# Two attention heads side by side on TensorE, the rope's swap of neighbours by DMA, and the causal mask filled into the probabilities by GpSimd

## What is computed

```python
# layer 0: deformable 3x3 convolution: 9 taps, each a bilinear sample at an offset that a 3x3 convolution gives
sampled = bilinear_sample(x, ys, xs)
out = einsum('bkhwc,ock->bohw', sampled, w) + bias
# layer 1: causal attention, 16 heads of 64, over the 1024 tokens of an image, with rope on q and k
q, k = apply_rope(x @ w_q.T), apply_rope(x @ w_k.T)      # pairs (a, b) -> (a*c - b*s, a*s + b*c)
out = softmax(mask(q @ k.T / 8)) @ v @ w_o.T
# layer 2: spectral filters (16 causal convolutions) and a mix of experts
```

## Time and profile before

| | |
|---|---|
| median of 3 runs | 3925.68 us (3906.31 to 3928.64) |
| span of the profiled execution | 3932.8 us |
| its offsets and convolution stages | up to about 290 us |
| its attention stage | about 292 to 3114 us |
| its spectral stage | from about 3118 us to the end |
| busy share of the span | PE 86%, DVE 63%, POOL 43%, ACT 37% |

### The profile page before, as it was taken

How to read it: one execution, slowest core, us unless ns; L and a number is a source line. 1 busy time by engine, 2 the same in 40 slices (tenths; PEclk the granted TensorE clock), 3 DMA queues, 4 the chain that set the end, 5 groups by cost and what they waited for, 6 DMA issues and landing times. The chain is left out here.

```text
span 3932.8 us, 69093 instructions
## 1 busy us (share of the span) xinstructions
PE 3385.7 (86%) x21387; PEld 2365.0 (60%) x21387; DVE 2484.0 (63%) x4247; ACT 1442.3 (37%) x2188; POOL 1702.7 (43%) x1424
## 2 busy tenths in 40 slices
PE   6336999999999999999999999999999569999998
PEld 1124555555555555555555555555555359898887
DVE  2346666676666767666766766667676556464646
ACT  0002333333333333333333333333333235454545
POOL 0464555555555555555555555555555320000000
PEclk8557999999999999999999999999999779999999
DMA  2524454445545544444554445455555624333333
GB/s 78 165 85 138 120 133 127 131 125 129 137 119 133 135 126 128 130 132 118 138 134 124 126 129 136 120 132 135 125 130 124 136 70 135 101 133 102 119 123 103
DMA packets 289629, 487.77 MB, mean 124 GB/s; under 512 B 95336, under 2 KB 113144, under 8 KB 289304
## 3 DMA queue, kind: packets, MB, share of 16 engines
q1 hardware_dynamic: 257160, 398.26, 36.8%
q0 software_dynamic: 32400, 88.52, 9.4%
HBM read 258.31 MB, written 23.27 MB: 72 GB/s over the span
## 5 line engine op out<-in xcount | busy, mean ns | idle before, releaser
L1108 ACT ACTIVATE attention_probs<-attention_pss 128x896 f32<-128x896 f32 (+4 forms) x768 | 623.0, 811 | 1320.9 <-PE attention_pss L957 1310.4
L1165 DVE TENSOR_REDUCE attention_mx<-attention_pss 128x2 f32<-128x1024 f32 (+3 forms) x520 | 525.5, 1022 | 377.8 <-PE attention_pss L970 208.1
L1041 PE MATMUL attention_psY<-attention_probs,attention_xt 128*64 128x128 f32 (+7 forms) x4386 | 733.5, 440 | 2.1 <-DMA attention_xt<-xt 1.8
L1283 POOL DMA_INDIRECT attention_gat<-table,attention_idx x585 | 559.8, 957 | 191.6 <-issue 118.8
L954 PE MATMUL attention_pss<-attention_QA,attention_KA 128*128 128x512 f32 (+4 forms) x1536 | 554.1, 416 | 49.5 <-ACT attention_probs L1108 43.7
L1696 DVE SCALAR_TENSOR_TENSOR spectral_eo<-spectral_psE,spectral_sig,spectral_eo 64x512 fp32r<-64x512 f32 x512 | 383.9, 750 | 263.8 <-ACT spectral_eo L1675 259.2
L1264 POOL TENSOR_TENSOR attention_nat_l<-attention_qk,attention_nat_h 128x512 fp32r<-128x512 f32 x260 | 425.3, 1636 | 259.3 <-ACT attention_nat_h L1127 259.3
L970 PE MATMUL attention_pss<-attention_nat_h 64*128 64x512 f32 (+2 forms) x1560 | 350.7, 451 | 201.7 <-DVE attention_mx L1165 198.2
L1599 PE MATMUL spectral_psE<-spectral_tz,spectral_up 128*128 128x256 f32 (+2 forms) x3072 | 507.5, 324 | 4.3 <-DVE spectral_eo L1696 4.3
L1256 POOL TENSOR_TENSOR attention_qk<-attention_tA,attention_tB 128x512 f32<-128x512 f32 x260 | 411.1, 1592 | 203.5 <-DVE attention_tB L1180 201.9
L1599 PEld LDWEIGHTS spectral_psE<-spectral_tz,spectral_up 128*128 128x128 f32 x3072 | 470.7, 188 | 44.9 <-DVE spectral_eo L1696 6.1
(11 more groups left out here) (194 smaller groups left out, 3862.4 us busy)
## 6 DMA issues: line engine op xcount, KB each, us to landing
attention_QA<-attention_nat_h SPq DMA_DIRECT2D x520, 128.0 KB
spectral_tz<-phis SPq DMA_DIRECT2D x128, 320.5 KB, 4.7
spectral_tz<-phis SPq DMA_DIRECT2D x128, 320.0 KB, 4.3
attention_xb<-xn SPq DMA_DIRECT2D x66, 512.0 KB, 4.0
attention_wt<-wsplit SPq DMA_DIRECT2D x66, 512.0 KB, 5.9
attention_KA<-attention_nat_h SPq DMA_DIRECT2D x260, 128.0 KB
attention_KB<-attention_nat_h SPq DMA_DIRECT2D x260, 128.0 KB
attention_KA<-attention_nat_l SPq DMA_DIRECT2D x260, 128.0 KB
```

The costliest lines, as they stand in the source:

```text
L1041: ins = pe.matmul(psY[C * half:C * half + C, c0:c1], xt[:, kt_, :], probs[:, q + c0:q + c1], start=first, stop=(j == NS - 1), skip_group_c ...
L1108: act.activation(probs[:, pstep[j]:pstep[j] + width], pss[:, slot, lead:lead + width], ACT.Exp, scale=float(E) ** -0.5).then_inc(s_act, 1)
L1165: ins = dve.tensor_reduce(mx_far[:, :, i - 4] if k0 else mx[:, :, i], scores, AX.X, ALU.max)
L1283: pool.indirect_dma_start(gat[:, n, :, :].rearrange("p q c -> p (q c)"), None, d.table.rearrange("r q c -> r (q c)"), bass.IndirectOffsetO ...
```

## The change

- **Both heads of a pair side by side.** `ORDER` now has 12 steps a pair, n = 0 to 11; step n starts with ("S", n % 2, n // 2), head n % 2 and key tiles `STEPS[n // 2]`. `pv` is done once for both heads: head 0 goes to PSUM partitions 0 to 63 and head 1 to 64 to 127, over all of a step's query columns. `yT` holds both heads, so that 8 matmuls of 130 columns in two units ("out", 0) and ("out", 1) take the place of 16 of 65 columns. `leave` is one instruction. `probs` keeps three of the six steps for each head.
- **Rope's swap by DMA.** The second set of weights is gone. ("rope", c), c = 0, 1, now makes keys and queries of 512 tokens in 4 matmuls. DVE multiplies with the swapped sin into `tB` first, SP carries `tB` to `qk` with even and odd partitions exchanged (`swap`, 2 DMAs of 128 KB, 64 partitions each), and POOL adds `tA` in place. `swap(r)` waits for `lower(r - 2)`, which reads the same buffer of `qk`.
- **The causal mask on POOL.** The L957 matmuls are gone. After exp, `causal` fills zeros above the diagonal of each 128x128 block of `probs`: 8 blocks a head, 16 a pair, one instruction each, one block in `mask` n of steps n = 0, 1 and 6 to 11, two in those of n = 2 to 5. `pv` waits for it.
- `UNITS`, `DEFORM_AT`, `UPPER_AT`, `PV_AT` and `POOL_ORDER` are new.

```diff
-MAX_OF = {"a": [(0, 0, 1)], "b": [(1, 0, 2)], "c": [(2, 0, 3)], "d": [(3, 0, 4)],
+MAX_OF = {"ac": [(0, 0, 1), (2, 0, 3)], "b": [(1, 0, 2)], "d": [(3, 0, 4)],
...
+UNITS = [
+    [("rope", 0)],
+    [("rope", 1)],
+    [("out", 0)],
+    [("out", 1)],
+    [("max", "b")],
+    [("max", "ac"), ("max", "d")],
+    [("max", "e"), ("dT",)],
+    [("max", "f"), ("max", "g"), ("dR",)],
+    [("max", "h"), ("max", "i")],
+    [("max", "j"), ("max", "k")],
+    [("row",)],
+    [("dX",)],
+]
...
-UPPER_AT = {1: [0, 1], 3: [2], 5: [3]}
+DEFORM_AT = {2: ["m0"], 3: ["m1", "m2"], 4: ["a0"], 5: ["a1"], 9: ["s"]}
+POOL_ORDER = [("mask", 0), ("mask", 1), ("add", 0), ("mask", 2), ("add", 1), ("mask", 3), ("lower", 0), ("add", 2),
+              ("mask", 4), ("lower", 1), ("add", 3), ("mask", 5), ("lower", 2), ("lower", 3), ("mask", 6), ("gather", 0),
+              ("token", 0), ("mask", 7), ("token", 1), ("mask", 8), ("gather", 1), ("mask", 9), ("gather", 2),
+              ("mask", 10), ("mask", 11)]
+UPPER_AT = {3: [0, 1], 4: [2, 3]}
+PV_AT = {2 * j + 3: j for j in range(NS - 1)}
+LAST_PV = 1
...
+                def swap(r, done, first=False):
+
+                    if not first or r > 1:
+                        wait_apart(sp, s_low, done + (r - 1), s_apart)
+                    wait_apart(sp, s_turn, done + (r + 1), s_apart)
+                    for odd in range(2):
+                        sp.dma_start(qk[odd:P:2, r % 2, :], tB[1 - odd:P:2, r % 2, :]).then_inc(s_swap[r % 2], 16)
...
+                            for r in range(4):
+                                swap(r, 8 * it + 4 * (1 + k))
...
-                            d0 = c0 + P * kt_ - q0
-                            ins = pe.matmul(out[:, d0:d0 + P], identb[:, :], mask_b[:, 0, :], start=False, stop=True,
-                                            skip_group_check=True)
...
-                        for a in range(2):
+                        for i in range(2):
+                            w = ROPE_OF[2 * c + i][0]
                             for part in range(2):
-                                ins = pe.matmul(out[:, a * HB:(a + 1) * HB], wt[:, pp, part, 2 * (1 - w) + a, :],
+                                ins = pe.matmul(out[:, i * HB:(i + 1) * HB], wt[:, pp, part, 1 - w, :],
                                                 xb[:, pp, c * HB:(c + 1) * HB], start=(part == 0), stop=(part == 1))
...
+                    pe.wait_ge(s_causal, 2 * NB * it + (NB * k + 2 * j + NB + 2))
...
+                    for kt_, at, c0, c1 in values(j):
+                        for h in range(2):
+                            ins = pe.matmul(psY[C * h:C * h + C, c0:c1], xt[:, kt_, :], probs[:, h, at + c0:at + c1],
+                                            start=(j == 0), stop=(j == NS - 1), skip_group_check=True)
...
+                        for i in range(2):
+                            r = 2 * u[1] + i
...
+                            dve.wait_ge(s_sum, R + r + 1)
+                            dve.tensor_tensor(tB[:, r % 2, :], pss[:, slot, i * HB:(i + 1) * HB], sinT[:, cols],
+                                              ALU.mult).then_inc(s_turn, 1)
+                            dve.tensor_tensor(tA[:, r % 2, :], pss[:, slot, i * HB:(i + 1) * HB], cosT[:, cols],
+                                              ALU.mult).then_inc(s_dve if i else s_cos, 1)
...
-                    pool.tensor_tensor(qk[:, r % 2, :], tA[:, r % 2, :], tB[:, r % 2, :], ALU.add).then_inc(s_sum, 1)
+                    pool.wait_ge(s_swap[r % 2], 64 * pair + 32 * (r // 2 + 1))
...
+                    pool.tensor_tensor(qk[:, r % 2, :], qk[:, r % 2, :], tA[:, r % 2, :], ALU.add).then_inc(s_sum, 1)
...
+                    for t in STEPS[j]:
+                        block = probs[:, h, at:at + P]
+                        ins = pool.affine_select(block, block, [[1, P]], ALU.is_ge, zero, base=0, channel_multiplier=-1)
+                        at += S - P * t
+                    ins.then_inc(s_causal, 1)
```

404 lines of the change are left out of this document (194 added, 210 removed).

## The result

The changed kernel takes **4403.08 us** (median of four runs, 4402.22 to 4407.92); the kernel before took 3916.21 beside it. The ratio is **1.1236**, 95% interval 1.12 to 1.1273: slower, as forecast, and 203 us above the forecast of 4200, inside its range. It is 487 us more than the kernel before, where 274 were forecast (4200 against 3926). The profiled execution has a span of 4406.2 us.

The account below looks back on a forecast made before the run. PE's own work was taken to set the pace at 43.1 us a pair; after the change a chain through the other engines would take 47.3. 3932.8 + 269 + 5, less 7, gave 4200 us, range 3975 to 4500.

Parts of the forecast that it names:

- What PE loses: PE's work in rope, output, mask matmuls and values: 5.2 us a pair less, leaving 34.1.
- ACT holds PE at upper 2 and upper 3: ACT's queue: both wait for POOL's adds ahead of the exp of step 5, so PE stands some 9.6 us.
- A swap at 2.6 us: Rope's DMA from tB to qk: each swap taken at 2.6 us, bounds 2.0 and 3.2.
- step 3: Chain from upper 0 through two swaps, adds and lowers to upper 3 and the exp: 12.6 to 26.95 us.
- Step 4: Chain behind PE's stand: POOL's masks 5 to 7, lowers, gathers and tokens' add, to 37.1 us; PE there at 35.4.
- Step 5: Chain's end: values, scores, last maxima, DVE's read of k and combining, normalisation, dX: 37.1 to 45.85 us.
- the handoffs: Between engines along the chain: some 20 at 0.07 us, 1.4 us a pair on top of the steps.
- PE stays the bound: Rival, 5%: add 3 done before PE needs the slot, at about 17.3 us, so the 5.2 are kept: 3593 us.
- The chain is there, but short: Rival, 6%: low prices, handoffs of 0.5 and swaps at 1.5 make a pair 41.9 us: 3854 us in all.
- The fill is slow: Rival, 10%: a fill on POOL takes 1 us a block, 5.0 us more a pair: 4520 us in all.
- The swap doesn't do what a copy does: Rival, 6%: rows of alternate partitions take 2 us more each, 4 us a pair: 4456 us in all.
- The clock stays low: Rival, 15%: PE's clock is low in the chain's step 5 too, 3.2 us more a pair: 4405 us in all.

Follow-up runs that it names:

- upper_late: The changed kernel with upper 2 moved behind step 5 and upper 3 behind step 7 in ACT's list, POOL's order kept; 4707.39 us.
- upper_pool: upper_late with POOL's order changed too: lower 2, mask 6 ahead of add 3, lower 3 behind it, mask 7 ahead of the gathers; 4254.09 us, ratio 1.085.
- no_swap: The changed kernel without the swap's DMAs; POOL adds tB and tA where they stand, so features are not exchanged; 4130.92 us.
- rope_matmul: The changed kernel with rope by matmuls as before in four units, no swaps; heads side by side and fills kept; 3807.08 us, ratio 0.9714.
- no_fill: The changed kernel with the causal fills taken out and nothing in their place; 4262.82 us.
- hybrid: rope_matmul with its maxima one place earlier and the mask of steps 2 and 3 back in PE, their 4 fills gone; 3821.84 us, ratio 0.9759.

## Why the prediction was right, and where its size was off

The pair of the timelines above, laid on the steps of the forecast (us from the start of its first scores at 1499.16):

| step | forecast | measured |
|---|---|---|
| 2: add 1 ends | 10.15 | 9.5 |
| 3: lower 0 ends | 15.1 | 14.4 |
| 3: add 2 ends | 19.3 | 19.1 |
| 3: add 3 ends | 25.4 | 25.1 |
| 3: exp of step 5 starts | 26.0 | 25.6 |
| 3: PE goes on | 26.95 | 26.6 |
| 5: values after mask 7 start | 37.1 | 37.9 |
| 5: dX | 45.55 | 47.9 |
| next pair | 47.3 | 49.2 |

- **What bounds it: right. What PE loses: less than forecast.** Its busy share in attention is 70%, forecast 72%, but of a longer pair: 0.704 x 50.4 = 35.5 us, where 34.1 was forecast. It fell by 3.8 us from 39.3 and not by 5.2; part of the rest is work at half clock.
- **ACT holds PE at upper 2 and upper 3: right**, in place and size. PE stood 9.2 us, forecast 9.6. upper_late, upper_pool and no_swap moved or shortened exactly this stand.
- **A swap at 2.6 us: too short.** POOL stood 3.02 us from the end of `lower` to the add, with the DMA as the releaser. Two of them, 0.8 us a pair. DVE's two-input work was seldom beside the adds, so these took 1.27 instead of 1.6, except add 2 (1.64); and the fill was 0.31, not 0.45. These errors cancel by luck: step 3 ends within 0.4 us. On the fill the Trainium skill (GPSIMD Engine Reference, Engine selection) was the better guide, with its line rate for one-input operations; by it the forecast would have been some 90 us less, further from the total.
- **Step 4, behind the stand: the wrong engine, and the low clock.** The forecast let POOL reach mask 7 last, at 37.1, with PE there at 35.4. POOL had mask 7 done at 35.95 (1535.11). PE's waits in attention name POOL nowhere; PE itself was late, at 37.9, because it worked at half clock for the first 6 us behind the stand. Its values in that stretch took 2.79 us, where the same 8 matmuls took 1.72 in rope_matmul. From the stand's end to the values after mask 7 it took 11.3 us; the forecast gave POOL 10.15 and PE 8.45.
- **Step 5, one reading left out.** The forecast has DVE read k and combine. It reads j first:

```profile
1540.16 2.42 DVE L1167 TENSOR_REDUCE attention_mx_far<-attention_pss 128x2 f32<-128x256 f32 x3 [1.44 <-PE attention_pss L975]
1542.62 0.17 DVE L1173 TENSOR_TENSOR attention_mx<-attention_mx,attention_mx_far 128x8 f32<-128x8 f32 x1
```

  2.42 us where 1.22 stood: 1.2 us a pair. The normalisation behind it took 4.0 us (forecast 3.83). This mistake needed no run: the order shows the units.
- **The clock: named, but put in the wrong place.** The forecast saw 2 us of room for it in step 4 and priced it only in step 5, as a rival. It was the other way round: it took that room and 1.15 us more in step 4, and step 5, from 1537.04 on, ran at 1.00. Besides, it was low at the opening of the next pair, as the 1.91 us for its rope show. The forecast has that nowhere. The opening takes 3.57 us at half clock (1548.38 to 1551.95, first scores to last values) and 2.06 at full clock, as in this pair (1499.16 to 1501.22): 1.5 us. The Trainium skill's rule on idle time (TensorE: Matmul & The Clock Gate, The HAM clock gate) agrees with 0.60 and 0.54 in and behind the stand, and with 1.00 once PE had worked again.

So the mechanism held and the sum was 3.1 us a pair short. In this pair 1.9: -0.35 up to the end of the stand, +1.15 for PE at low clock in step 4, +1.2 for the reading left out, +0.35 for the normalisation and what lies around it, -0.45 for the handoffs, put at 1.4 in the forecast and in part contained in the steps here.

The mean pair (50.4) takes 1.2 more than this one, and two things go into it, which were counted but not tested. This pair has an opening at full clock, which is rare: of the 61 pairs in which the timeline shows the four rope matmuls of the opening by themselves, they took 1.55 to 1.91 us in 57 and 1.09 in 4. And the last ten of the 63 intervals between the copies of L1107 average 52.9 us, the other 53 average 49.9. In those last ten PE waits at the opening for the DMA of the maxima's row, a path that the forecast let end 1 us ahead of the other (PE's wait in 3005 to 3605 us):

```profile
PE attention_pss L953 <- DMA attention_QB<-attention_rows_b: 28.5, 10, 3.8
```

Of the rivals, "PE stays the bound" (3593) fell: it needed add 3 by 17.3 us, and it came at 25.1. "The chain is there, but short" (3854) fell with 50.4 us a pair. "The fill is slow" fell at 0.315 us in this kernel, and rope_matmul shows when a fill is longer (below). "The swap doesn't do what a copy does" fell at 3.02. "The clock stays low" (4405) came nearest to the number by luck: it has the low clock in step 5, where the clock was full.

## What to carry to other kernels

- Work taken off the engine that sets the pace helps only while the chain through the others is shorter than what is left. Here PE's busy time fell by 3.8 us a pair, and a chain with a DMA of 3.0 us in it twice put 9.2 us of idle time in its place; without the DMA 4.2 of the 9.2 stayed. Add up that chain before moving arithmetic to a DMA.
- In lists that each engine walks in order, an instruction that waits holds all behind it, also where it takes 0.3 us itself. Moving a wait means reading the lists of both engines; upper_late and upper_pool differ in POOL's list alone and by 453 us.
- Split a change before judging it. Three edits came as one at +12%; without the swap, and with the maxima in a better place, the other two give -5.4%.

## What was not expected of the hardware

A fill's time depends on what DVE does. In the changed kernel it took 0.315 us in the mean. In rope_matmul the same instruction took 505 ns in the mean; the group, and two places where it stands beside DVE's products on gathered rows and beside its sum of them (2 in 1.97 us, 1 in 1.41):

```profile
L1279 POOL TENSOR_SCALAR_AFFINE_SELECT attention_probs<-attention_probs 128x128 f32<-128x128 f32 x1024 | 506.1, 505 | 467.4 <-ACT attention_probs L1093 464.0
```

```profile
1509.82 1.97 POOL L1279 TENSOR_SCALAR_AFFINE_SELECT attention_probs<-attention_probs 128x128 f32<-128x128 f32 x2
...
1512.99 1.41 POOL L1279 TENSOR_SCALAR_AFFINE_SELECT attention_probs<-attention_probs 128x128 f32<-128x128 f32 x1
```

It works the other way too, and these rows show an order in it. DVE in the pair of the changed kernel shown above, beside POOL's rows there:

```profile
1510.97 0.95 DVE L1198 TENSOR_TENSOR attention_gat<-attention_gat,conv_Wc 128x768 f32<-128x768 f32 x1
...
1512.39 2.86 DVE L1198 TENSOR_TENSOR attention_gat<-attention_gat,conv_Wc 128x768 f32<-128x768 f32 x2
...
1515.77 1.34 DVE L1201 TENSOR_TENSOR attention_gat<-attention_gat 128x1152 f32<-128x1152 f32 x1
```

- POOL's two fills of 1511.41 start within the product of 1510.97. They take 0.91 us instead of 0.54; the product takes 0.95, the same as in no_fill with POOL idle.
- `lower` 0 starts at 1512.29, 0.1 us ahead of the next two products. It takes 1.27, its usual time, and they take 2.86 instead of 1.9.
- add 2 starts at 1516.59, within the sum of 1152 gathered elements. It takes 1.64 instead of 1.27; the sum takes 1.34, the same as in no_fill with POOL idle for most of it.
- In hybrid (rows above) `lower` starts 0.03 us behind the first of two products, and there it is `lower` that is long, 2.06; the second product is then held, 2.90 for both.

In these four places the instruction that starts second is the one that gets longer, by somewhat less than what the first still has to run. The sum takes 1.75 us in rope_matmul and 2.00 in hybrid, where the end of a `lower` that started first covers its first 0.5 and 0.8 us, with fills behind; in the kernel before, beside POOL's adds and lowers all the way, it takes 2.31. So a short one-input instruction on POOL isn't free of DVE's two-input work; that a fill delays DVE is not shown by these rows, since a `lower` is there each time that DVE's sum is longer.
